# State space layer: GpSimd scales the output, spreads C in one pass per group and takes the remainder's difference

## The reference

```python
def _mamba(xt, in_proj, conv_w, conv_b, x_proj, dt_w, dt_b, A_log, Dp, out_w, out_b):
    xz = xt @ in_proj
    xc, z = (xz[..., :D_INNER], xz[..., D_INNER:])        # 256 each
    xp = jnp.pad(xc, ((0, 0), (D_CONV - 1, 0), (0, 0)))
    xconv = conv_b
    for kk in range(D_CONV):                              # 4 taps in time
        xconv = xconv + conv_w[:, kk] * xp[:, kk:kk + T, :]
    xc = jax.nn.silu(xconv)
    dbc = xc @ x_proj
    dt = jax.nn.softplus(dbc[..., :DT_RANK] @ dt_w + dt_b)
    Bm, Cm = ...                                          # 16 states
    dA = jnp.exp(dt[..., None] * A)
    dBx = (dt * xc)[..., None] * Bm[:, :, None, :]
    # scan over time: h = dA_t * h + dBx_t;  y_t = sum over states of h * C_t
    y = jnp.swapaxes(ys, 0, 1) + Dp * xc
    y = y * jax.nn.silu(z)
    return y @ out_w + out_b
...
xt = layernorm(xt + _mamba(xt, ...), nt_g, nt_b)
```

## Time and profile before

| | |
|---|---|
| median of 3 runs | 3863.41 us (3857.32 to 3867.41) |
| span of the profiled execution | 3864.4 us |
| scans of the state space layer | 495.3 to 2099.1 us of the span, 512 of them |
| VectorE in all scans (L1246) | 1141.5 us busy, 2270 ns each |
| GpSimd, busy over the span | 2377.3 us (62%) |
| VectorE, busy over the span | 2993.7 us (77%) |
| TensorE, busy over the span | 3158.9 us (82%) |

### The profile page before, as it was taken

The page is one execution under the profiler, slowest core; times in us unless marked ns, Lnnn a source line. Parts: engine busy times, 40 slices in busy tenths (PEclk is TensorE's granted clock), DMA queues, the critical chain, the costliest instruction groups (busy, mean ns, idle before and its releaser), DMA issues. The chain is left out here.

```text
span 3864.4 us, 82478 instructions
## 1 busy us (share of the span) xinstructions
PE 3158.9 (82%) x29152; PEld 2183.1 (56%) x29152; DVE 2993.7 (77%) x5896; ACT 2599.8 (67%) x5235; POOL 2377.3 (62%) x2879
## 2 busy tenths in 40 slices
PE   7999589999999999999986876688848856678486
PEld 3766356666666666666664563366636533456455
DVE  3999579999999999999997567389858663278754
ACT  4888489999999999999984210266756363077562
POOL 2899588898898999988874000177755130044850
PEclk7999799999999999999999568677769867789698
DMA  3000100000000000000000512501000014500424
GB/s 93 24 24 26 51 4 13 24 24 24 24 24 24 24 22 17 20 24 24 23 18 23 145 40 93 207 23 29 7 5 1 1 25 142 189 5 1 121 56 126
DMA packets 271007, 172.53 MB, mean 45 GB/s; under 512 B 41648, under 2 KB 249977, under 8 KB 268537
## 3 DMA queue, kind: packets, MB, share of 16 engines
q1 hardware_dynamic: 270600, 167.25, 15.1%
HBM read 116.59 MB, written 50.60 MB: 43 GB/s over the span
## 5 line engine op out<-in xcount | busy, mean ns | idle before, releaser
L1246 DVE TENSOR_TENSOR_SCAN mam_hs<-mam_dA,mam_ps_b 128x1024 f32<-128x1024 f32 x512 | 1141.5, 2270 | 80.9 <-issue 44.0
L1162 ACT ACTIVATE mam_dA<-mam_dt,mam_A 128x496 f32<-128x496 f32 x1024 | 658.7, 710 | 0.4
L1018 PE MATMUL mam_ps_h<-mam_ident,mam_hs 128*128 128x128 f32 x4096 | 549.6, 277 | 61.2 <-ACT mam_hTb L1170 30.8
L1018 PEld LDWEIGHTS mam_ps_h<-mam_ident,mam_hs 128*128 128x128 f32 x4096 | 454.0, 142 | 226.9 <-issue 149.2
L1170 ACT COPY mam_hTb<-mam_ps_h 128x512 f32<-128x512 f32 x768 | 424.5, 589 | 95.9 <-PE mam_ps_h L1018 95.9
L1004 PE MATMUL mam_ps_b<-mam_DB,mam_dtxt 32*128 32x512 f32 x2048 | 292.5, 638 | 77.6 <-DVE mam_hs L1246 73.6
L1031 PEld LDWEIGHTS mam_ps_y<-mam_hTb,mam_WC 128*32 128x32 f32 x8192 | 208.9, 109 | 133.2 <-issue 124.3
L1031 PE MATMUL mam_ps_y<-mam_hTb,mam_WC 128*32 128x128 f32 x8192 | 276.7, 275 | 0.3 <-issue 0.3
L780 POOL TENSOR_TENSOR mam_cv<-mam_cv,mam_tap 128x512 f32<-128x512 f32 x180 | 239.1, 1328 | 14.1
L816 POOL TENSOR_TENSOR mam_WC<-mam_cp,mam_m 128x128 f32<-128x128 f32 x512 | 194.6, 411 | 19.9 <-POOL mam_cv L780 14.8
L1256 DVE COPY mam_hTb<-mam_ps_h 128x512 f32<-128x512 f32 x256 | 174.3, 681 | 37.9 <-PE mam_ps_h L1018 35.9
(11 more groups left out here) (738 smaller groups left out, 8290.4 us busy)
## 6 DMA issues: line engine op xcount, KB each, us to landing
moe_wg<-in_L_ffn_weight SPq DMA_DIRECT2D x32, 1024.0 KB, 8.2
rnn_xr<-x SPq DMA_DIRECT2D x23, 512.0 KB, 5.7
l1y_wh<-mode_weights SPq DMA_DIRECT2D x16, 544.0 KB, 3.7
gat_hg<-in_x SPq DMA_DIRECT2D x16, 512.0 KB, 7.1
h<-gat_out SPq DMA_DIRECT2D x32, 256.0 KB, 2.3
mam_ht<-h SPq DMA_DIRECT2D x128, 64.0 KB, 2.0
mam_hr<-h SPq DMA_DIRECT2D x128, 64.0 KB, 2.0
mam_xt<-in_x SPq DMA_DIRECT2D x128, 64.0 KB, 2.0
```

Of the source, the lines that this page charges most:

```text
L1018: last = pe.transpose(ps_h[n][:, q * P:(q + 1) * P], hs[:, w % 3, c:c + P], ident[:, :])
L1162: act.activation(dA[:, h, :, n, 1:], dt[:, i % 2, h, :].rearrange("p (q t) -> p q t", q=Q)[:, :, 1:], ACT.Exp, scale=A[:, h, n:n + 1]).the ...
L1246: dve.tensor_tensor_scan(hs[:, w % 3, :], dA[:, h, first:first + 2, :, :].rearrange("p q s t -> p (q s t)"), ps_b[:, 2 * (w % 2):2 * (w % ...
```

## The change

- `scale(i)` moves from VectorE (u = 15 of turn i+1) to GpSimd (u = 3 of turn i+2, between `spread_c` and `gate`); `residual` on VectorE now waits for the `scale` of the turn before, since `z` and the means have one buffer.
- `spread_c` makes its four operations of 128x128 into one over [P, J, S4, T], 512 elements per partition.
- In the softplus, VectorE only subtracts one: e = ln - 1. The difference with dt moves to GpSimd's `time_steps`: e = dt - e, followed by dt = ln + e, with a new semaphore `lost_ready` between the two.
- `plus` adds a broadcast column of ones as a tensor, instead of the immediate 1.0.

```diff
+        one_c = s.sb("one", [P, 1])
...
+            step(pool.memset(one_c[:, :], 1.0))
...
-                pool.tensor_scalar(ln[:, h, :], e[:, h, :], 1.0, None, ALU.add).then_inc(e1_ready, 1)
+                pool.tensor_tensor(ln[:, h, :], e[:, h, :], one_c[:, :].broadcast_to([P, N]), ALU.add
+                                   ).then_inc(e1_ready, 1)
 
             def time_steps(i, h):
-                pool.wait_ge(rest_ready, 2 * i + h + 1)
-                pool.wait_ge(ln_ready, 2 * i + h + 1)
-                pool.tensor_tensor(dt[:, i % 2, h, :], ln[:, h, :], e[:, h, :], ALU.subtract
-                                   ).then_inc(dt_ready, 1)
+                n = 2 * i + h
+                pool.wait_ge(rest_ready, n + 1)
+                pool.tensor_tensor(e[:, h, :], dt[:, i % 2, h, :], e[:, h, :], ALU.subtract).then_inc(lost_ready, 1)
+                pool.wait_ge(ln_ready, n + 1)
+                pool.wait_ge(lost_ready, n + 1)
+                pool.tensor_tensor(dt[:, i % 2, h, :], ln[:, h, :], e[:, h, :], ALU.add).then_inc(dt_ready, 1)
...
-                for j in range(J):
-                    last = pool.tensor_tensor(
-                        WC[:, j, g, :, :], cp[:, i % 2, j, g, :].unsqueeze(2).broadcast_to([P, S4, T]),
-                        m32[:, :].unsqueeze(1).broadcast_to([P, S4, T]), ALU.mult)
-                last.then_inc(WC_ready, 1)
+                every = [P, J, S4, T]
+                pool.tensor_tensor(WC[:, :, g, :, :], cp[:, i % 2, :, g, :].unsqueeze(3).broadcast_to(every),
+                                   m32[:, :].unsqueeze(1).unsqueeze(1).broadcast_to(every), ALU.mult).then_inc(WC_ready, 1)
...
+            def scale(i):
+                pool.wait_ge(rstd_ready, i + 1)
+                if i >= 1:
+                    pool.wait_ge(stored, 16 * J * i)
+                for g in range(G):
+                    last = pool.tensor_scalar(out[:, g, :], z[:, g, :], mv[:, g, 0:1], rstd[:, g:g + 1],
+                                              ALU.subtract, ALU.mult)
+                last.then_inc(scaled, 1)
...
+                if u == 3 and turn(k - 2):
+                    scale(k - 2)
...
-                STT(out=e[:, h, :], in0=ln[:, h, :], scalar=1.0, in1=dt[:, i % 2, h, :], op0=ALU.subtract,
-                    op1=ALU.subtract).then_inc(rest_ready, 1)
+                TS(e[:, h, :], ln[:, h, :], 1.0, None, ALU.subtract).then_inc(rest_ready, 1)
...
+                if i >= 1:
+                    dve.wait_ge(scaled, i)
...
-            def scale(i):
-                dve.wait_ge(rstd_ready, i + 1)
-                if i >= 1:
-                    dve.wait_ge(stored, 16 * J * i)
-                for g in range(G):
-                    last = TS(out[:, g, :], z[:, g, :], mv[:, g, 0:1], rstd[:, g:g + 1],
-                              ALU.subtract, ALU.mult)
-                last.then_inc(scaled, 1)
...
-                if u == 15 and turn(k - 1):
-                    scale(k - 1)
```

More of the change, by code:

```diff
@@ L665, in mamba @@
         (loaded, made, prepared, folded, turned, hT_ready, xc_done, xc_ready, conv_first, conv_ready, cols_in, xs_ready, gate_done, sz_ready,
-         bc_done, bc_ready, dt_made, dt_read, e_ready, e1_ready, ln_ready, plus_ready, rest_ready, dt_ready, dtx_ready, cp_done,
+         bc_done, bc_ready, dt_made, dt_read, e_ready, e1_ready, ln_ready, plus_ready, rest_ready, lost_ready, dt_ready, dtx_ready, cp_done,
          cp_ready, dx0_done, dx0_ready, dx1_done, dx1_ready, DB_ready, WC_ready, dA_ready, b_done, scanned, flipped,
@@ L672, in mamba @@
                 "xs_ready", "gate_done", "sz_ready", "bc_done", "bc_ready", "dt_made", "dt_read", "e_ready", "e1_ready",
-                "ln_ready", "plus_ready", "rest_ready", "dt_ready", "dtx_ready", "cp_done", "cp_ready", "dx0_done", "dx0_ready",
+                "ln_ready", "plus_ready", "rest_ready", "lost_ready", "dt_ready", "dtx_ready", "cp_done", "cp_ready", "dx0_done", "dx0_ready",
                 "dx1_done", "dx1_ready", "DB_ready", "WC_ready", "dA_ready", "b_done", "scanned", "flipped",
```

## The result

The changed kernel takes 3932.2 us (median of 4 runs, 3922.93 to 3944.46) against 3862.0 for the kernel before on the same chip: ratio 1.0188, interval 1.0171 to 1.0205. Its profiled span is 3932.3 us, 67.9 more than before. That is slower, as forecast, but 35 us above the predicted time and 4 above its range.

A forecast was written before the change was run, and what follows sets the result against it. The prediction took GpSimd's stretch into the second Silu as the binding chain: 1.75 - 0.42 - 0.13 = +1.20 us in 28 turns, plus 0.6, made +34.2 on 3863.4, so 3897.6; range 3864 to 3928.

The forecast's parts named there:

- The place: GpSimd's stretch from first convolution to the second Silu is the binding chain; a late convolution is paid one to one.
- GpSimd's addition costs little: Rival: the added GpSimd work costs 0.4 us or less per turn; at 0.25 the time is 3871; chance 0.12.
- VectorE as the bound: Rival: VectorE, with the highest busy share, sets the time; 33 us would come back, giving 3831; chance 0.10.
- the price of the scaling: Term in GpSimd's stretch: four tensor_scalar of `scale` at 0.44 each by L4228, 1.75 us in all.
- the upper bound of 2.25: Upper bound for the four scalings on GpSimd: 4 x 0.56, by the single operation at L2926.
- the rest of the sum: Terms beside the scaling's 1.75: -0.42 and -0.13 make +1.20 us in 28 turns; with +0.6 at the end, +34.2.
- `spread_c`: Term in GpSimd's stretch: four operations in 1.47 us become one pass of about 1.05, saving 0.42; at worst 0.19.
- Sharing with VectorE: Term in GpSimd's stretch: two meetings with VectorE's subtractions at 0.10 each against 0.33 now, -0.13; bounds -0.33 and +0.33.
- The doubling rule: Skill's rule that elementwise work is about twice as slow on GpSimd: `scale` 2.4 us, total an estimated 3916.
- `time_steps`: New GpSimd subtractions, 2.7 us per turn, cost 0: the first ends 0.33 before the decay; at worst 0.3 per turn.
- The subtraction becomes the wait as well: Rival: decays start 0.3 late and upper bounds hold, 2.7 per turn, +75, giving 3939; chance 0.06.
- VectorE's share: Sign: VectorE's busy share falls from 94% by 6 to 9 points.

The follow-up runs named there:

- with the addition: Changed kernel with add, mult in place of subtract, mult in GpSimd's scaling: 3889.9 (one run) beside 3856.2 for the kernel before.
- with two passes: Changed kernel with the scaling on GpSimd as two 128x512 passes with broadcast operands: 3911.5, ratio 1.0145 to the kernel before.
- with the passes alone: Kernel before with only the one-pass `spread_c` and `plus` as a tensor add of one: 3853.8, ratio 0.9990.
- those with the pauses: Changed kernel with GpSimd waiting for its own result after each half of `gate`: 3980.7, ratio 1.0297 to the kernel before.
- at its later place: Changed kernel with `z`, means and `rstd` in two buffers and `scale` on GpSimd at u = 11, right before `finish`: 3860.1, ratio 1.0012.
- The two runs with an addition: Changed kernel with the scaling as add, mult: 3889.9 beside 3856.2; or as mult, add with a negated product: 3890.3 against 3867.4, ratio 1.0059.

## Why the prediction was right, and where it was wrong

- **The place.** Right. GpSimd's stretch into the second Silu is the chain, and what is added there is paid for one to one: the medians of stretch and turn were 21.50 and 50.43 before, 22.57 and 51.40 with the addition, 23.08 and 51.90 with two passes, 23.94 and 52.76 after: turn = stretch + 28.8 in the three in which the Silu waits, + 28.9 before. Below some 21.4 the turn stays at 50.2, which is why the shorter stretches, with the scaling back on VectorE or with the passes alone, hardly show in the time. The rule ends where TensorE's clock falls: the longer turns of the scaling's move alone and those with the pauses are some 1.5 us above it. The rival "GpSimd's addition costs little" is out, and so is VectorE as the bound: neither the scaling off VectorE (at its later place) nor the split difference gave a turn below 50.2, and 28.8 holds alike with VectorE's subtraction at a mean of 1.06 us (the addition) and of 1.74 (after).
- **The step that failed: the price of the scaling.** "I take 1.75, since the form agrees": the form didn't agree. L4228 of the earlier trace rows multiplies and then adds; `scale` subtracts and then multiplies. The scalings cost 0.79 each, 3.13 in a turn, where the term said 1.75, and the upper bound of 2.25, from the immediate operation of the earlier trace rows, was too low as well. The difference, 1.38 us in each of 28 turns, is 39 us, where the time came out 35 above the forecast. The bound was taken for one over all operations of that size, and it stood on one row; the kernel before has no tensor_scalar with a subtraction on GpSimd, so no row of it could have shown the price. The two runs with an addition test the rest of the sum: their 28 turns are 27 and 28 us longer together, and their times 34 us (one execution) and 23 us (15 to 31) above the kernel before, against 34.2 in the sum. So the rest stands to within some 7 us, and that the one execution hits 34 is luck.
- **The other terms.** `spread_c`: 1.05 from 1.47, -0.42 as said. Sharing with VectorE: 0.07 twice, against 0.33 once, -0.19 for a term of -0.13. With the measured price, 3.13 - 0.42 - 0.19 = +2.52 by the terms, against +2.48 in the stretch of the turn shown and 2.44 in the median. The turn grew by 0.1 less than the stretch (2.33 in the median), which the sum, counting the stretch whole, left out; the 28 turns make 66 of the 70 us.
- **The doubling rule.** The estimate by the Trainium skill (GPSIMD Engine Reference, Performance versus the Vector engine), 2.4 us, lies between the two forms: 1.74 with the addition, 3.13 with the subtraction. The page's measured factor, 1.96, is for a two-input addition; against VectorE's 1.19 the scaling shows 1.5 and 2.6, so neither form bears the rule out.
- **`time_steps`.** Right. L801 ends at 1265.33 + 1.27 = 1266.60 and the decay starts at 1266.89: 0.29 to spare, where 0.33 was worked out. "The subtraction becomes the wait as well" did not come about, though its time (3939) is near the one measured: the right time for the wrong reason.
- **VectorE's share.** Missed. I took the one-input subtraction to be shorter; it is 0.42 us by itself, but takes up to 2.43 with the wait for GpSimd. It cost nothing in time, since VectorE isn't the chain. I had the row for it (L580's maximum) and used it only for what GpSimd loses.

## What to carry to other kernels

Price an operation that goes to another engine by a row with the same ALU operations, not only the same form and size; where there is none, let the upper bound reach further than the nearest row. Before work is moved, look for the stretch on the new engine that someone waits for, and put the work behind its end: here the place alone was worth 70 us of 3862. And a cure for one wait can be dearer than the wait, if it leaves a third engine idle and that engine comes back at a lowered clock.

## What the runs showed of the hardware

- GpSimd's tensor_scalar on 128x128 with two operands per partition takes 0.45 us as add, mult or mult, add, and 0.79 to 0.80 as subtract, mult or mult, subtract. As tensor_tensor the subtraction costs no more: 1.27 like an addition on full operands, 1.04 on a broadcast one. Why is open.
- VectorE's one-input subtraction took from 0.42 to 2.43 us for the same work. In the changed kernel it ended 0.20 us behind the first gap between GpSimd's operations, and where it started as GpSimd came out of a pause it took 0.42; scalings under GpSimd's `plus` went from 1.11 to 2.81. GpSimd lost 0.07 in each meeting of the changed kernel, but 0.29 (1.56 instead of 1.27) in the one where the subtraction started with it. A gap alone isn't the rule: among those scalings one of 1.31 us ended 0.08 behind the end of one operation of GpSimd, when the next had already started (1049.68 to 1050.99; L790 ended at 1050.90, L792 began at 1050.87). The Trainium skill (SBUF — State Buffer, Who interferes with whom) has the two engines exclude each other for whole instructions where VectorE is in a two-port mode; the trace agrees that it is a wait, and adds that VectorE bears nearly all of it while GpSimd's operations follow without a pause.
- TensorE's granted clock fell to 0.52 and 0.55 after idle times of 3.07 and 1.95 us, and to 0.70 and 0.65 after 1.72 us in two turns of the two-pass run. It stayed full after 1.93 in a neighbouring turn, after 1.68 in nearly all turns of the changed kernel, and there also after 2.68, 2.69 and 3.01. A turn in which it fell is some 1.5 us longer. The length of the idle time alone doesn't decide; what does is open.
